# Three edits to an attention kernel: the masked bias product moved ahead, the maxima turned one tile later, the causal value product in one piece

## The reference

```python
def _L2_cond_ref(x, t, mask, ...):
    m = mask[:, :, None]
    norm = jnp.where(m, layernorm(x) * (1.0 + scale) + shift, 0.0)
    fwd = gelu(norm @ ssm_w1 + ssm_b1) @ ssm_w2 + ssm_b2
    bwd = flip(gelu(flip(norm) @ bwd_w1 + bwd_b1) @ bwd_w2 + bwd_b2)
    x = x + gate_msa * jnp.where(m, fwd + bwd, 0.0)     # the bias counts only where m holds
    ...
def _attention(...):                                     # L1 (no mask) and L3 (causal)
    scores = einsum('bhqd,bhkd->bhqk', q, k) * scale
    scores = where(causal, scores, -inf)                 # L3 only
    out = einsum('bhqk,bhkd->bhqd', softmax(scores), v)
```

## Time and profile before

| | |
|---|---|
| median of 3 runs | 489.45 us (487.57 to 489.74) |
| the profiled execution | 488.39 us, its span 486.6 us |
| PE busy | 317.5 us, 65% |
| DVE busy | 303.9 us, 62% |
| ACT busy | 251.0 us, 52% |
| POOL busy | 121.9 us, 25% |
| mean granted TensorE clock | 0.825 |

### The profile page before, as it was taken

One profiled execution on the slowest core, in us unless ns is written; L12 is line 12 of the kernel. 1 busy time (PEld: TensorE's weight loads), 2 busy tenths in 40 slices (PEclk: granted clock), 3 DMA queues, 4 the chain that ended last, 5 costly groups with the idle time before them and its releaser, 6 DMA issues.

```text
span 486.6 us, 6451 instructions
## 1 busy us (share of the span) xinstructions
PE 317.5 (65%) x2274; PEld 148.4 (31%) x2274; DVE 303.9 (62%) x683; ACT 251.0 (52%) x550; POOL 121.9 (25%) x184
## 2 busy tenths in 40 slices
PE   0015844621245563988988888758678977788786
PEld 0004613511103420222222345535222232333354
DVE  0778787759588659888888314346675354554230
ACT  3267645562466212788887773333435354456542
POOL 0112139640363510000000202563012222222410
PEclk9999965555557756799999999989757598889799
DMA  7940350000000233000000000000710000000001
GB/s 243 417 186 0 130 223 0 1 0 0 1 0 1 68 99 92 2 3 3 1 2 2 2 2 1 0 1 20 198 43 2 1 2 3 2 1 2 1 1 43
DMA packets 11652, 21.90 MB, mean 45 GB/s; under 512 B 2010, under 2 KB 10462, under 8 KB 10846
## 3 DMA queue, kind: packets, MB, share of 16 engines
q1 hardware_dynamic: 11620, 21.49, 12.8%
HBM read 14.54 MB, written 0.52 MB: 31 GB/s over the span
## 4 chain that ended last, share of the span: by engine, by line
PE 41%; DVE 24%; ACT 18%; POOL 6%; issue 6%; DMA 2%; SPq 2%; DVEq 0%; ACTq 0%; POOLq 0%
PE pe L1475 10%; ACT big L1173 8%; PE pe L1497 6%; DVE nm L932 5%; PE pe L1376 4%; PE pe L1529 4%; PE pe L1451 4%; PE pe L1454 3%; PE pe L1247 2%; POOL rstd L344 2%; ACT scr L1058 2%; PE pe L1341 2%; PE pe L1426 1%; DVE st L516 1%; DVE xn L526 1%
## 5 line engine op out<-in xcount | busy, mean ns | idle before, releaser
L1173 ACT ACTIVATE big<-pe 128x512 f32<-128x512 f32 (+3 forms) x256 | 116.7, 521 | 81.6 <-PE pe L1497 80.4
L932 DVE TENSOR_REDUCE nm<-pe 128x2 f32<-128x1024 f32 (+2 forms) x112 | 124.2, 1145 | 50.1 <-PE pe L1454 38.1
L1475 PE MATMUL pe<-big,scr 128*32 128x256 f32 (+4 forms) x896 | 74.1, 408 | 3.8 <-ACT scr L1146 2.6
L1451 PE MATMUL pe<-big 62*128 62x512 bf16 (+3 forms) x256 | 53.1, 395 | 15.9 <-DVE nm L932 13.0
L1497 PE MATMUL pe<-big 64*128 64x512 bf16 (+3 forms) x256 | 54.9, 371 | 8.4 <-ACT big L1173 7.0
L344 POOL TENSOR_TENSOR rstd<-var,half 128x4 f32<-128x4 f32 x26 | 28.5, 1097 | 110.5 <-DVE var L521 85.9
L440 POOL TENSOR_SCALAR_AFFINE_SELECT big<-big 128x512 f32<-128x512 f32 x32 | 20.3, 635 | 73.4 <-ACT big L1173 73.4
L1497 PEld LDWEIGHTS pe<-big 64*128 64x128 bf16 x256 | 15.7, 94 | 64.7 <-ACT big L1173 33.5
L430 POOL CAST nm<-nm 128x16 bf16<-128x16 f32 x16 | 3.1, 196 | 102.0 <-DVE nm L932 102.0
L526 DVE TENSOR_SCALAR xn<-x_tok,mv,rstd 128x128 f32<-128x128 f32 x64 | 18.6, 353 | 15.7 <-POOL rstd L344 15.7
L1475 PEld LDWEIGHTS pe<-big,scr 128*32 128x32 f32 x896 | 18.9, 111 | 29.2 <-issue 12.3
(11 more groups left out here) (188 smaller groups left out, 560.3 us busy)
## 6 DMA issues: line engine op xcount, KB each, us to landing
big<-tern SPq DMA_DIRECT2D x48, 128.0 KB, 2.4
big<-in_fill SPq DMA_DIRECT2D x1, 4096.0 KB, 13.6
big<-in_wa SPq DMA_DIRECT2D x1, 2304.0 KB, 12.5
w<-in_w SPq DMA_DIRECT2D x2, 1152.0 KB, 19.2
big<-in_wa SPq DMA_DIRECT2D x1, 1344.0 KB, 6.2
big<-in_w SPq DMA_DIRECT2D x1, 1024.0 KB, 14.4
w<-in_w SPq DMA_DIRECT2D x1, 896.0 KB, 19.8
rowg<-in_rowg SPq DMA_DIRECT2D x1, 832.0 KB, 18.4
```

Source lines behind the costliest of these rows:

```text
L932: v.tensor_reduce(dst, src[:, :, 0:w * len(pairs)].rearrange("p r (h w) -> p r h w", w=w), AX.X, ALU.max, negate=True).then_inc(sem(f"a{a} ...
L1173: s_.activation(P[:, kt % PRING, 2 * p + j, q0:S], bank[SINGLES[i % 3]][:, q0:S], ACT.Exp, scale=SCALE).then_inc(sem(f"a{a}_p"), 1)
L1451: last = t_.matmul(dsts[par][:, k * wd:(k + 1) * wd], QZ[rows, b, 2 * g + i, qt * 128:(qt + 1) * 128], KZ[rows, b, 2 * g + i, 0:wd], start ...
L1475: last = t_.matmul(bank[PV_BANK][32 * h:32 * h + 32, lo:hi], V[b][:, kt, HG * g + h, :], P[:, k % PRING, h, lo:hi], start=(kt == 0), stop= ...
```

## The change

Line numbers of the code after are lower than those before by 3 to 6 from `add_bias` on (L1475 is L1470, L1497 is L1492, L1451 is L1445, L1421 is L1415, L398 is gone).

```diff
-        LAG = 1
-        LATE = (3, 4)
+        LAG = 2
+        LATE = (3, 5)
...
-            ahead = n + n // 2
+            ahead = n + n // 2 + 1
...
+            mask_bias = row0[:, 0:B * TB * D].rearrange("p (t d) -> p t d", d=D)
+
             def add_bias(n, b):
                 pool.wait_ge(sem("n_xn"), B * n + b + 1)
-                if n == 2:
-                    for t in tiles(b):
-                        link(nc.gpsimd.tensor_scalar(junk[:, 0:D], gate_bias(n, b), maskf[:, t:t + 1], None, ALU.mult))
-                        last = nc.gpsimd.tensor_tensor(x_tok[:, t], x_tok[:, t], junk[:, 0:D], ALU.add)
-                        link(last)
-                    pool.sem_inc(sem("n_bias"), 1)
-                else:
-                    nc.gpsimd.tensor_tensor(x_tok[:, bt(b)], x_tok[:, bt(b)], wide(gate_bias(n, b)),
-                                            ALU.add).then_inc(sem("n_bias"), 1)
+                bias = mask_bias[:, bt(b)] if n == 2 else wide(gate_bias(n, b))
+                nc.gpsimd.tensor_tensor(x_tok[:, bt(b)], x_tok[:, bt(b)], bias, ALU.add).then_inc(sem("n_bias"), 1)
...
                     n_root(n, b)
-                    if n != 2:
-                        add_bias(n, b)
+                    add_bias(n, b)
...
+                if n == 0:
+                    for t in range(B * TB):
+                        link(nc.gpsimd.tensor_scalar(mask_bias[:, t], gate_bias(2, t // TB), maskf[:, t:t + 1], None, ALU.mult))
...
-                if n == 2:
-                    for b in range(B):
-                        add_bias(n, b)
...
-                        lo, hi = (q0, S if kt == 0 else mid) if part == 0 else (mid, S)
-                        if kt == 0 and part == 1:
+                        whole = kt == 0 or causal
+                        lo, hi = (q0, S if whole else mid) if part == 0 else (mid, S)
+                        if whole and part == 1:
                             return
...
-                                             P[:, k % PRING, h, lo:hi], start=(kt == 0), stop=(kt == TB - 1 and part == 1),
+                                             P[:, k % PRING, h, lo:hi], start=(kt == 0), stop=(kt == TB - 1 and (part == 1 or causal)),
                                              tile_position=(0, 32 * h))
-                        last.then_inc(sem(f"a{a}_pv"), 2 if kt == 0 else 1)
+                        last.then_inc(sem(f"a{a}_pv"), 2 if whole else 1)
```

## The result

The changed kernel took **483.17 us** (median of 4 runs, 480.48 to 486.88), the kernel before 489.01 beside it: a ratio of 0.989 (95% interval 0.985 to 0.992). The forecast was 477 and 0.975. So the change is faster, but by 2 to 6 us and not by 12.

What follows compares the result with a forecast made beforehand. The bound changes by stage: three engines in the first attention, TensorE with its idle places in causal units, GpSimd's bias between stages. -3.8 - 0.3 + 1.5 - 6.6 - 3.0 = -12.2 us from 488.39 gives 476.2, forecast 477, range 467.5 to 484.

Steps and rivals of the forecast that it cites:

- Part 1: Between stages n = 2 and 3: GpSimd's masked bias taken ahead of time lets `normed` start sooner, -3.8 us (-3.5 to -4.1).
- The rival in which the bias was not the last wait: Between stages n = 2 and 3: the masked bias wins only 1.2 us, whole time 480; chance 0.03.
- Parts 2 and 3: Attention starts +1.1 and +1.5 us; first attention's tail -1.4 as `out` stops waiting; first attention with its start -0.3.
- Part 4: Six causal units: 1.25 us less per unit at full clock, 1.1 taken, so -6.6 us (bounds -2.6 and -14.9).
- The first two terms: In a causal unit: TensorE's 0.72 us wait for a reduction goes, and 0.10 us more beside the merged products' saving.
- (c): Causal units win the pieces alone: parts' slack gone, or (second condition) scores wait for exponentials; 483 us; chance 0.18.
- the pieces: Causal units: merging value products into 384 columns saves 0.14 us for each of three key tiles, 0.43 us a unit.
- the sum above with the clock as patchy as now: Whole kernel, likeliest case (a): all parts summed with the clock unchanged, 477 us (472.5 to 481); chance 0.50.
- part 5: Causal tail: no `out` wait and merged key tiles, half-clock stretch as now, -3.0 us (-1.1 for the wait alone, -4.2).
- The prediction's own sign of being wrong: Causal units' clock below 0.8 in most; also slot 8 scores waiting for `nmp`, or first attention over 1 us longer.
- (b): Clock stays up in causal units, five at 10.6 us: units -14.1, tail -4.2, time 468.5; chance 0.17.
- (e): Slower: idle places keep half clock in every causal unit, 14.2 us each, +6.7, tail wins nothing, 493.5; chance 0.05.

Runs made afterwards that it cites:

- the second profile: The changed kernel timed again without any edit: 487.5 us (485.81 to 488.52), ratio 0.995 to the kernel before.
- one piece alone: Kernel before with only the causal value product in one piece and LATE (3, 5) instead of (3, 4): 495.51 us, ratio 1.012.
- before, copy later: Kernel before with only ScalarE's copy of a causal unit's sum two half slots later: 480.14 us, ratio 0.980.
- before, filled: Kernel before with eight unread products ahead of each causal parts wait and eight between the scores of a unit's slot 4: 479.59 us, ratio 0.980.
- changed, four slots: Changed kernel with LATE (3, 4) instead of (3, 5), the late products at four slots instead of five: 475.63 us, ratio 0.973.
- changed, filled: Changed kernel with eight unread products ahead of each causal parts wait and eight between the scores of a unit's slot 4: 472.7 us, ratio 0.966.
- changed, copy later: Changed kernel with ScalarE's copy of a causal unit's sum two half slots later: 469.57 us, ratio 0.959.

## Why the prediction was right and wrong

**Part 1, the masked bias: right, a little small.** Forecast -3.8; the stage is 4.4 us shorter with it, in the whole change and alone, and the time 5.5. The rival in which the bias was not the last wait is out: the kernel without this part (490.92) stands 3.4 to 7.8 us above the one with it. The cover of the eight products held.

**Parts 2 and 3: right in kind.** The start cost 0.9 of the 1.1 us forecast, the causal one 0.8 (and 0.3 up to the first mark) of 1.5. The `out` in the first tail lost its wait, and the attention is 2.2 us shorter from its first scores on, so -1.3 together against -0.3. The 0.8 us beyond the 1.4 of `out` were costed at nothing. The first attention's waits for the parts, 0.30 to 0.39 us before, are gone from the trace too, but no run shows that they are the 0.8.

**Part 4, the units: the mechanism right, the size not.** At full clock the forecast was 0.72 + 0.10 + 0.43 = 1.25 us; measured 11.85 - 11.10 = 0.75. The six units won 5.1 us in the first profile, and in the second nothing (78.97 for 78.49). The first two terms are there: TensorE's idle time in a unit fell from 11.85 - 9.30 = 2.55 to 11.11 - 9.33 = 1.78. The 384 columns take 404.37 - 403.59 = 0.78 us, as the prediction had it (the line itself gives 0.76), so the 0.14 us that do not depend on the columns are real. But TensorE's *busy* time did not fall by the 0.43 (9.30 and 9.33). It is used up at the scores: 0.77 us for the second pair at 405.13, while the first at 404.37 took 0.39. The even slots have no value product now, so the second score of a pair meets an exponential that is not over yet, and a wait between two instructions of a group is shown as their duration. The row at 405.50 shows it: the second score's weights are loaded only when ScalarE's exponential releases them. That is rival (c)'s second condition, worth 0.77 - 0.39 = 0.38 us a unit at full clock, nearly the whole of the pieces. No run took these waits away alone. The prediction also left out that the attention's last parts now stand in the sixth unit, where TensorE waits 0.48 and 0.43 us more (431.58 and 432.34 below). The term of the sum for the reduction was put to the wrong edit: with `LAG` alone 0.45 of the 0.72 us stay, with the later whole products alone none.

**The step that failed is the clock**: "the sum above with the clock as patchy as now", and in part 5 "the same half-clock stretch as now". I priced each idle place as so many us of waiting and held the clock constant. In this kernel the clock is more than half of what an idle place costs: the copy moved in the kernel before takes 0.73 us from a full-clock unit, 4.4 us in six, and 9.7 us from the time. The prediction's own sign of being wrong, a clock below 0.8 in most units, is there in the second profile (four of six). The column "units, tail" is the time of the six units and the tail in the profiled execution; the sixth unit of the kernels with `LAG` = 2 also holds the wait for the last parts:

| kernel | idle places in a unit, us | clocks of the units | unit at 1.00 | units, tail | time |
|---|---|---|---|---|---|
| one piece alone | 0.89, 0.95 | 0.75 in five of six | none | 102.98 | 495.51 |
| before | 0.89, 0.95, 0.72 | 0.66 to 1.00 | 11.85 | 97.88 | 489.45 |
| changed | 0.89, 0.85 | 0.69 to 1.00 | 11.10 | 94.28, 99.59 | 483.17, 487.5 |
| before, copy later | 0.16, 0.95, 0.71 | 1.00 and 0.86 by turns | 11.12 | 88.94 | 480.14 |
| before, filled | 0.34, 0.42, 0.72 | 1.00 in five of six | 11.74 | 89.11 | 479.59 |
| changed, four slots | 0.72, 0.85, 0.45 | 1.00 and 0.87 by turns | 11.56 | 89.22 | 475.63 |
| changed, filled | 0.34, 0.31 | 1.00 in five of six | 11.11 | 86.12 | 472.7 |
| changed, copy later | 0.85 | 0.75, 0.86, then 1.00 | 10.24 | 83.55 | 469.57 |

The longest idle place in a unit is 0.95 us. Two of 0.85 to 0.95 close together take the clock down in most units; 0.95 and 0.71 farther apart do it in every other unit; with one of 0.85 alone it rises from 0.75 in the first unit over 0.86 to 1.00 and stays there to the tail. A rule by length and number alone doesn't come out: with four slots the idle places add up to 2.02 us and with five to 1.74, and the clock is the better one with four. The Trainium skill, "TensorE: Matmul & The Clock Gate", section "A second HAM failure mode: psum-queue depth-cycling", tells of a kernel in which TensorE is idle only briefly, but often, between groups of matmuls, and its clock falls and rises over and over. The trace agrees, with idle places of 0.85 to 0.95 us and units at 0.66 to 0.87.

That the clock and not the idle time itself is at work is shown by the filler, which leaves the full-clock unit as it is and gives 10 us and more. (No run put the useless products anywhere but in idle places; the moved copy, which adds no work, brings the clock up as well.) That it hid part of the change's gain is shown by the pair with the later copy: 10.6 us between them, against 2 to 6 us as the kernels stand. That this is near the forecast sum of 12.2 is in part luck. Between the two profiles, cut at the first `o_turn` of the tail in both, the units give -5.7 us (forecast -6.6), the tail +0.3 (forecast -3.0), and all ahead of the units -5.1 (forecast -2.6).

The rivals' numbers are luck too where they fit. (c) said 483, and 483.17 was measured, but with units at -5.1 for its -2.6 and a tail at +1.5 for its -1.5. (b), the clock that stays up, said 468.5; the kernel that meets its condition is the filled one, with 472.7, in the main since its unit is 11.11 and not 10.6 us. The 469.57 of the later copy is another kernel, with a unit of 10.24, in which the wait that (b) left standing is gone. (e) was right in kind for one part of the change: the one piece alone has a half-clock stretch in every unit and is slower. But its units cost 2.4 us more than before (13.6 us each, not 14.2) and its tail 2.8, where (e) had +6.7 and nothing. With the maxima's edit beside it the time is that of the kernel before (490.92), and only with the bias too is it below. The one piece with the bias alone was not run.

**Part 5, the causal tail: wrong sign.** Forecast -3.0, measured +1.5 and +1.2. With the clock equal on both sides (0.81 and 0.82, both kernels filled) the tail gains 19.16 - 17.97 = 1.2 us, about the 1.1 that the lower bound had for `out` alone. So of the 4.5 us missed, some 1.8 were a sum made too large and 2.7 are the clock (0.69 for 0.82), which now falls to half at the tail's `o_turn`, `out` and 512 columns. What stands ahead of that stretch are three idle places; before, only the last of them was there. In the changed kernel:

```profile
431.58 0.33 PE L1492 MATMUL pe<-big 64*128 64x384 bf16 x1 [0.48 <-ACT big L1167]
432.34 0.22 PE L1415 MATMUL pe<-cmask,nm 128*32 128x128 bf16 x1 [0.43 <-POOL nm L429]
...
433.89 0.39 PE L1492 MATMUL pe<-big 64*128 64x256 bf16 x1 [0.91 <-ACT big L1167]
434.22 1.11 PE L1427 MATMUL pe<-ident,xn 128*128 128x128 f32 x4
```

In the changed kernel with the copy later, the third is gone, and `o_turn` runs at full clock (0.66 us, as before the change at 443.29), `out` (0.66) and the 512 columns (1.06) behind it too:

```profile
423.93 0.33 PE L1492 MATMUL pe<-big 64*128 64x384 bf16 x1 [0.48 <-ACT big L1167]
424.69 0.22 PE L1415 MATMUL pe<-cmask,nm 128*32 128x128 bf16 x1 [0.43 <-POOL nm L429]
...
425.27 0.66 PE L1427 MATMUL pe<-ident,xn 128*128 128x128 f32 x4
```

The units ahead of it had run at 1.00, so it isn't shown that the third place alone decides. The second stretch at half clock, near the tail's end, stands in the kernel before and in both of these (512 columns in 1.93 or 1.94 us at 456.51, 449.94 and 437.88) and was not taken apart.

What stays open, then, is the rest of the tail, and why units of the same kernel with the same idle places differ in clock from one execution to the next (changed kernel: 73.42 and 78.97 us for six units). Nothing in the instructions differs between them.

## What to carry to other kernels

Before pricing an edit in a stage whose granted clock is below 1.00, price the idle places of TensorE twice, as waiting and as clock. Look for the one that another engine's order makes: moving one copy on ScalarE by two half slots gave the kernel before 9.7 us, where the three edits studied here gave 2 to 6. A merge that takes work from TensorE without closing the idle places can be slower, as the one piece alone was. A quick test of whether the clock is the limit is to fill the idle places with products that nobody reads. Where repeats of a kernel differ by more than those of its base (480.48 to 488.52 against 487.57 to 491.16), one profile of it is not its profile.

## What the runs showed of the hardware

Useless products made both kernels faster, by 10 us before and by 10 to 15 after, with all useful work unchanged. And the mean granted clock of a whole run says little of its time: the kernel before took 488.97 us at a mean of 0.818 and 488.99 at 0.922. The kernel with the maxima's edit alone had a mean of 0.919 and took 486.78 us; its first 100 us, against those of the kernel before, were

```profile
0.00:100.00 100.00, 40.93 (x166) 28.30 (x166) 69.01 (x192) 54.21 (x130) 33.64 (x46) 1.00 0.37 146
```

```profile
0.00:100.00 100.00, 39.40 (x166) 27.42 (x166) 69.37 (x193) 54.71 (x130) 34.40 (x46) 0.82 0.37 146
```

(the second of the kernel before). TensorE does the same 166 instructions there at 1.00 and at 0.82, and is not what that part waits for; only the clock in the stretches that TensorE bounds counts.
